# Both one-hots of an edge-to-node kernel made by bf16 matmuls of integer rows and one ScalarE Relu each

## The reference

```python
q, k, v = x @ Wq + bq, x @ Wk + bk, x @ Wv + bv
e = edge_attr @ We
k_e, v_e = k[src] + e, v[src] + e
alpha = einsum(q[dst], k_e) / sqrt(16)            # per head
attn = softmax of alpha over the edges of one dst
out = segment_sum(attn * v_e, dst)
x_r = x @ Wskip + bskip
beta = sigmoid([out, x_r, out - x_r] @ Wbeta)
out = beta * x_r + (1 - beta) * out
return layernorm(x + x + relu(layernorm(out) * gamma + beta_ln))
```

## Time and profile before

| | |
|---|---|
| median of three executions | 2535.12 us |
| span of the profiled execution | 2124.7 us |
| so outside the span, by the median | 410.4 us |
| busy: PE, DVE, ACT, POOL | 74%, 85%, 53%, 71% of the span |
| DMA engines busy, mean | about three quarters of the main loop |

### The profile page before, as it was taken

The page is one execution under the profiler, slowest core; times in us unless marked ns, Lnnn a source line. Parts: engine busy times, 40 slices in busy tenths (PEclk is TensorE's granted clock), DMA queues, the critical chain, the costliest instruction groups (busy, mean ns, idle before and its releaser), DMA issues. The chain is left out here.

```text
span 2124.7 us, 43320 instructions
## 1 busy us (share of the span) xinstructions
PE 1580.3 (74%) x10903; PEld 1429.2 (67%) x10903; DVE 1807.1 (85%) x3704; ACT 1121.3 (53%) x3755; POOL 1502.4 (71%) x1586
## 2 busy tenths in 40 slices
PE   7678788778776777777776777777777777877763
PEld 5577777668676666666675776667666767767652
DVE  6687787788878888888888898898898999999985
ACT  1154445445445545555555555566555665666656
POOL 0377777777777777777777777777777777777750
PEclk9898899998999999999999989999999999899985
DMA  8887787777777777777777777777777777777741
GB/s 297 280 246 233 233 240 235 236 233 236 222 215 212 218 216 214 222 211 218 221 215 225 216 223 217 222 226 221 215 223 225 226 224 228 224 226 219 228 128 36
DMA packets 298207, 467.63 MB, mean 220 GB/s; under 512 B 49766, under 2 KB 192826, under 8 KB 297862
## 3 DMA queue, kind: packets, MB, share of 16 engines
q1 hardware_dynamic: 222552, 259.24, 39.7%
q0 software_dynamic: 75408, 205.58, 33.7%
HBM read 413.96 MB, written 50.66 MB: 219 GB/s over the span
## 5 line engine op out<-in xcount | busy, mean ns | idle before, releaser
L742 POOL DMA_INDIRECT kv<-kv_tab,src_all x1498 | 1425.4, 952 | 480.9 <-issue 443.4
L851 PE MATMUL e_ps<-we,ea 128*128 128x128 f32 x3136 | 472.2, 301 | 278.4 <-DVE kve L1437 271.8
L851 PEld LDWEIGHTS e_ps<-we,ea 128*128 128x128 f32 x3136 | 417.7, 208 | 324.5 <-DVE kve L1437 175.6
L1437 DVE TENSOR_TENSOR kve<-kv,e_ps 128x768 f32<-128x768 f32 (+1 forms) x392 | 421.6, 1084 | 214.8 <-DMA kv<-kv_tab,src_all 214.0
L1095 ACT ACTIVATE dist_en<-iota_n,neg_rel 128x128 bf16<-128x128 f32 x1568 | 500.0, 396 | 46.3 <-issue 46.3
L1119 ACT ACTIVATE wt_ps<-logit,used_b 128x64 f32<-128x64 f32 x196 | 62.3, 318 | 831.3 <-issue 692.0
L969 PE MATMUL sum_ps<-wv,hot_en 128*128 128x136 f32 x3136 | 466.4, 303 | 11.8 <-DVE wv L1487 4.6
L969 PEld LDWEIGHTS sum_ps<-wv,hot_en 128*128 128x128 f32 x3136 | 429.7, 209 | 31.9 <-issue 31.9
L864 PE MATMUL q_ps<-q_win,hot_ne 128*128 128x128 f32 x3136 | 420.6, 292 | 0.9 <-DMA q_win<-q_tab 0.9
L864 PEld LDWEIGHTS q_ps<-q_win,hot_ne 128*128 128x128 f32 x3136 | 407.3, 210 | 1.2 <-DMA q_win<-q_tab 1.2
L1458 DVE TENSOR_REDUCE logit<-prod 128x64 f32<-128x1024 f32 x196 | 239.2, 1220 | 19.4 <-issue 0.4
(11 more groups left out here) (144 smaller groups left out, 1237.9 us busy)
## 6 DMA issues: line engine op xcount, KB each, us to landing
ea<-eaT SPq DMA_DIRECT2D x196, 512.0 KB
row_b<-rel_row SPq DMA_DIRECT2D x196, 256.0 KB
q_win<-q_tab SPq DMA_DIRECT2D x392, 64.0 KB
kv<-kv_tab,src_all POOLq DMA_INDIRECT x1498
sum_tab<-sums SPq DMA_DIRECT2D x391, 59.5 KB
kv_tab<-tab_buf SPq DMA_DIRECT2D x33, 384.0 KB, 3.7
logit<-sum_tab SPq DMA_DIRECT2D x49, 136.0 KB
xt_buf<-xT SPq DMA_DIRECT2D x33, 192.0 KB, 4.0
```

The costliest lines, as they stand in the source:

```text
L742: pool.indirect_dma_start(out=head_rows(q) if u == t == 0 else kv[:, s, t, :], out_offset=None, in_=kv_tab[:, :], in_offset=bass.IndirectO ...
L851: mm = pe.matmul(e_ps[u][:, t * P:(t + 1) * P], ea[:, par, (u * TILES_G + t) * P:(u * TILES_G + t + 1) * P], we[:, :], start=True, stop=True)
L1437: dve.tensor_tensor(kve[:, s, a:TILES_G, :, :], kv[:, s, a:TILES_G, :].rearrange("p t (a c) -> p t a c", a=2), e4[:, a:TILES_G, :, :].to_b ...
```

## The change

Nothing of the result changes; the one-hots are made in another way. With r the relative number of an edge and n the number of a node, 1 - (r - n)^2 is 1 where they agree and at most 0 elsewhere, so its Relu is the one-hot. It is made by matmuls of bf16 rows whose products are exact: r, and r^2 in two parts (`rel_tab`, three rows in HBM in place of one), with two rows of ones below (`rel5`), against five rows of n (`node5`).

- `nearness(q,u)`: one matmul 3x128 by 3x512 into `q_ps[u]`, after `products(q-1,u)` has read that bank. `node_one_hot` moves to ScalarE: Relu of `q_ps` with a bias in a column (`near_b`) into `hot_ne`, which has two buffers for four. `q_spread` then overwrites the bank.
- `edge_nearness(q,u)`: four matmuls 5x128 by 5x128 into `e_ps[u]`, after `keys_values(q,u)` has read it. `edge_one_hot` is one Relu of `e_ps`. `edge_part(q+1,u)` waits for that Relu, no longer for `kve`.
- VectorE loses `node_one_hot`; ScalarE loses its Abs operations; `load_row` brings 3x1024 numbers in place of a broadcast to 128 partitions. Its buffer is read last by `edge_nearness`, so `load_row(q+1)` waits for `edge_nearness(q-1)`; before it waited for `node_one_hot(q-1)`, which VectorE made in step q-3.
- In the table stage ScalarE squares `rel_rows` twice, VectorE makes the rest (`rel_lo`) and the node rows, SyncE stores three rows for one.

```diff
             def load_row(q):
                 if q >= 2:
-                    sp.wait_ge(hotne_ok, 2 * q - 2)
-                sp.dma_start(row_b[:, q % 2, :], rel_row[:, q * PAIR:(q + 1) * PAIR].to_broadcast([P, PAIR])
-                             ).then_inc(row_ld[q % 2], 16)
+                    sp.wait_ge(near_ok, 2 * q - 2)
+                    sp.wait_ge(dist_mm, 2 * q - 2)
+                sp.dma_start(rel3[:, q % 2, :], rel_tab[:, q * PAIR:(q + 1) * PAIR]).then_inc(row_ld[q % 2], 16)
...
+            def nearness(q, par, u, i):
+                g = 2 * q + u
+                if u == 0:
+                    pe.wait_ge(row_ld[par], 16 * (i + 1))
+                if q:
+                    pe.wait_ge(prod_ok, g - 1)
+                pe.matmul(q_ps[u][:, :], node3[:, :], rel3[:, par, u * EDGES_G:(u + 1) * EDGES_G], start=True, stop=True
+                          ).then_inc(near_ok, 1)
+
+            def edge_nearness(q, par, u):
+                g = 2 * q + u
+                pe.wait_ge(kve_ok, kve_count(g))
+                for t in range(TILES_G):
+                    mm = pe.matmul(e_ps[u][:, t * P:(t + 1) * P],
+                                   rel5[:, par, (u * TILES_G + t) * P:(u * TILES_G + t + 1) * P], node5[:, :],
+                                   start=True, stop=True)
+                mm.then_inc(dist_mm, 1)
...
                 if not last:
                     for u in range(2):
+                        edge_nearness(q, par, u)
+                    for u in range(2):
                         edge_part(q + 1, 1 - par, u, i + par, False)
+                        nearness(q + 1, 1 - par, u, i + par)
...
             def edge_one_hot(q, par, u, reuse):
                 g = 2 * q + u
-                act.wait_ge(disten_ok, g + 1)
+                act.wait_ge(dist_mm, g + 1)
                 if reuse:
                     act.wait_ge(sum_ok, g - 3)
-                act.activation(hot_en[:, 2 * par + u, :, :], dist_en[:, u, :, :], ACT.Relu, bias=1.0, scale=-1.0
+                act.activation(hot_en[:, 2 * par + u, :, :].rearrange("p t n -> p (t n)"), e_ps[u][:, :], ACT.Relu
                                ).then_inc(hoten_ok, 1)
+
+            def node_one_hot(g):
+                act.wait_ge(near_ok, g + 1)
+                if g >= 2:
+                    act.wait_ge(q_ok, g - 1)
+                act.activation(hot_ne[:, g % 2, :], q_ps[g % 2][:, :], ACT.Relu, bias=near_b[:, :]).then_inc(hotne_ok, 1)
...
-                edge_distance(q, 0, first == 0)
-                edge_one_hot(q, par, 0, first is None or first >= 2)
-                edge_distance(q, 1, first == 0)
+                for u in range(2):
+                    edge_one_hot(q, par, u, first is None or first >= 2)
                 unit_part(q)
+                if q + 1 < PAIRS:
+                    for u in range(2):
+                        node_one_hot(2 * q + 2 + u)
...
                 weights(q, par, q - LAG + 1 if first is None else 1, first is None or first >= 2)
-                edge_one_hot(q, par, 1, first is None or first >= 2)
...
                 weighted(q, par, reuse)
-                if ahead:
-                    node_one_hot(q + 2, par, i + 1)
                 unit_part(q)
```

More of the change, by code:

```diff
@@ L188, in build @@
         ea = sb("ea", [P, 2, 2 * EDGES_G])
-        row_b = sb("row_b", [P, 2, 2 * EDGES_G], BF16)
+        rel5 = sb("rel5", [BOTH_K, 2, 2 * EDGES_G], BF16)
+        rel3 = rel5[0:NEAR_K, :, :]
+        node5 = sb("node5", [BOTH_K, P], BF16)
+        node3 = node5[0:NEAR_K, :]
+        node_near = sb("node_near", [BOTH_K, P])
+        node_hi = sb("node_hi", [BOTH_K, P], BF16)
+        node_two = sb("node_two", [BOTH_K, P])
+        pick = sb("pick", [BOTH_K, 4])
+        node_sq = sb("node_sq", [P, 1])
+        near_b = sb("near_b", [P, 1])
         q_win = sb("q_win", [P, 4, C])
-        hot_ne = sb("hot_ne", [P, 4, EDGES_G])
-        dist_en = sb("dist_en", [P, 2, TILES_G, P], BF16)
+        hot_ne = sb("hot_ne", [P, 2, EDGES_G])
         hot_en = sb("hot_en", [P, 4, TILES_G, P])
@@ L248, in build @@
         g_put = sb("g_put", [P, 1], I32)
+        rel_sq = kve[0:PAIRS // 2, 0:2, :, :, :].rearrange("p s t a c -> p (s t a c)")
+        rel_hi = hot_en[0:PAIRS // 2, 0:2, :, :].rearrange("p s t n -> p (s t n)").bitcast(BF16)
+        rel_lo = hot_en[0:PAIRS // 2, 2:4, :, :].rearrange("p s t n -> p (s t n)").bitcast(BF16)
         dst_rows = logit[0:PAIRS // 2, 0:2 * PAIR].bitcast(I32)
@@ L282, in build @@
         eps_b = sb("eps_b", [P, 1])
-        near_b = part(EDGES_G // 2).bitcast(BF16)
         q_ahead = part(Q_ROUNDS, TB, C)
@@ L347, in build @@
         hotne_ok = sem("hotne_ok")
-        disten_ok = sem("disten_ok")
+        dist_mm = sem("dist_mm")
         negm_ok = sem("negm_ok")
@@ L351, in build @@
         denom_ok = sem("denom_ok")
-        rowid_ok = sem("rowid_ok")
+        square_ok = sem("square_ok")
+        node3_ok = sem("node3_ok")
+        near_ok = sem("near_ok")
         sums_ok = sem("sums_ok")
@@ L529, in _ @@
                 if r == 10:
-                    sp.wait_ge(row_cast, 1)
-                    sp.dma_start(rel_row.rearrange("one (p j) -> (one p) j", j=2 * PAIR), rel_rows[:, :]
-                                 ).then_inc(rel_st, 16)
+                    for k, rows in enumerate((rel_rows[:, :], rel_hi, rel_lo)):
+                        sp.wait_ge(row_cast, k + 1)
+                        sp.dma_start(rel_tab[k:k + 1, :].rearrange("one (p j) -> (one p) j", j=2 * PAIR), rows
+                                     ).then_inc(rel_st, 16)
             def load_nodes(r):
@@ L988, in _ @@
             with pe.If(grouped):
+                pe.wait_ge(node3_ok, 2)
                 for u in range(2):
+                    nearness(0, 0, u, 0)
                     edge_part(0, 0, u, 0, True)
                 for u in range(2):
-                    q_spread(0, 0, u, 0, True)
+                    q_spread(0, 0, u, 0)
+                for u in range(2):
+                    edge_nearness(0, 0, u)
                 for u in range(2):
                     edge_part(1, 1, u, 0, False)
+                    nearness(1, 1, u, 0)
                 biases_made()
@@ L1077, in _ @@
             act.copy(neg_rel[:, :], dst_all[:, :]).then_inc(cast_ok, 1)
+            act.wait_ge(row_cast, 1)
+            act.activation(rel_sq, rel_rows[:, :], ACT.Square).then_inc(square_ok, 1)
+            act.activation(rel_hi, rel_rows[:, :], ACT.Square).then_inc(row_cast, 1)
             act.wait_ge(first_mm, 1)
@@ L1244, in step @@
                 weights(q, par, q - LAG + 1 if first is None else 1, first is None or first >= 2)
-                edge_one_hot(q, par, 1, first is None or first >= 2)
             with act.If(grouped):
+                act.wait_ge(rel_st, 16 * NEAR_K)
+                act.wait_ge(node3_ok, 2)
+                for u in range(2):
+                    node_one_hot(u)
                 for q in range(ROUND):
@@ new lines, in _ @@
+            dve.wait_ge(square_ok, 7)
+            dve.scalar_tensor_tensor(node_two[:, :], node_hi[:, :], pick[:, 1:2], node_two[:, :], ALU.mult, ALU.add
+                                     ).then_inc(square_ok, 1)
+            dve.wait_ge(square_ok, 8)
+            dve.scalar_tensor_tensor(node5[:, :], node_near[:, :], pick[:, 2:3], node_two[:, :], ALU.mult, ALU.add
+                                     ).then_inc(node3_ok, 1)
+            dve.wait_ge(row_cast, 2)
+            dve.tensor_tensor(rel_lo, rel_sq, rel_hi, ALU.subtract).then_inc(row_cast, 1)
@@ L1587, in unit_part, with step @@
                     mix(u)
-            def step(q, par, i, first=None, ahead=True):
+            def step(q, par, i, first=None):
                 reuse = first is None or first >= 2
@@ L1602, in step @@
                 weighted(q, par, reuse)
-                if ahead:
-                    node_one_hot(q + 2, par, i + 1)
                 unit_part(q)
             with dve.If(grouped):
-                dve.tensor_copy(row_id, part_id[:, :]).then_inc(rowid_ok, 1)
-                dve.wait_ge(rowid_ok, 1)
-                for q in range(2):
-                    node_one_hot(q, q, 0, False)
                 for q in range(ROUND):
@@ L1632, in _ @@
                 for q in range(PAIRS - ROUND, PAIRS):
-                    step(q, q % 2, q // 2, ahead=q + 2 < PAIRS)
+                    step(q, q % 2, q // 2)
                     if q == PAIRS - 3:
```

66 lines of the change are left out of this document (37 added, 29 removed).

## The result

The changed kernel takes 3254.8 us, median of four executions (3243.8 to 3276.7), against 2534.8 us before: a ratio of 1.285, 95% interval 1.280 to 1.290. The prediction was 2550 us, with 2578 as its upper end. The sign was right; the time was wrong by 700 us.

The account below looks back on a forecast made before the run. GpSimd's gathers were taken to bound the kernel from first to last. Table stage +5, main-loop removals 0, new loop +11, step 194 +1.1, VectorE's end -1.5: +15.6, taken as +15 on 2535.1, 2550 us; range 2537 to 2578.

Parts of the forecast that it names:

- Outside the span lie 410.4 us, which I leave as they are: Whole kernel: 410.4 us of the 2535.1 us median lay outside the 2124.7 us span and were left unchanged.
- the cover of 8.7 us: Main loop: VectorE can be some 8.7 us late before a gather waits, at no cost except at the end.
- if the time outside the span moves: Stated sign of being wrong: the 410.4 us outside the span would change; no size was given.
- Table stage: Before the gathers: added VectorE work and stores cost +5 us, between +1 and +8; first gather at 85 us for 79.8.
- Gathers, +0: Main loop: last gather's start less the first stays 1962 us; above 1975 the loop would be the bound for long.
- Behind the last gather: End of the kernel: the end comes 94 us after the last gather's start, where it was 82.7 us.
- The places in a step: Main loop, from T, the start of `products(q,0)`: Exp at T + 4.0, `weighted` at T + 4.45, `top_row` at T + 6.6.
- The half clock: TensorE's loop: two sets of work at half clock now stand on the path, about +0.3 us a step.
- the forecast's own case: Steps 166 to 193 take 10.45 us through TensorE and ScalarE, +11 us late at the end; 2550 us, chance 0.44.
- TensorE's loop is the bound for long: Rival, chance 0.24: 43 steps with `make_queries` at 10.6 us give +12, the last 28 +22, table +5: 2574 us.
- The rival by occupancy: Rival, chance 0.02: VectorE, the engine with the highest occupancy, is the bound; each 1.21 us saved counts, 2300 us.
- I am wrong if the clock rises: Stated sign of being wrong, on TensorE in the main loop: its clock rises; no size was given.

## Why the prediction was wrong, and where it was right

**The step that failed: "Outside the span lie 410.4 us, which I leave as they are".** They were inside. The page showed an execution in which signals were prompt, the times came from executions in which they were late, and I took a difference of 19% for a fixed cost. With it went the first sentence, that GpSimd is held from the first gather to the last, and the cover of 8.7 us: in the timed executions GpSimd waited for TensorE at each pair (2.25 us at 1502.28). The prediction named the sign ("if the time outside the span moves") but did not price it.

**Where the 720 us come from.** Before, with late signals, a pair is 8.76 us from the first to the last start of its eight gathers, 0.94 for the last one, 1.84 until VectorE gets its signal, and 0.45 to the next gather: 11.99. `edge_part`, for which VectorE waits, and `q_spread`, for which GpSimd waits, were done by then; only their signals were missing. After, `hot_ne` on ScalarE needs the signal of `nearness`, and `q_spread` can only start behind it: 8.74 + 0.95 for the gathers, 1.74 to the signal, 0.84 until TensorE begins, 3.62 of `q_spread` at half clock, 0.26 to the next gather: 16.15. The difference is 4.2 us in the pair read, of which the hand-over is 0.84 and `q_spread` 3.62 (1.95 to 2.05 at full clock, so some 1.6 are the clock). 720 / 196 = 3.7 on the mean of all pairs. Shown are the lateness in rows of gathers, that it goes with plain loads, and that pace shortens it; the division in hand-over and clock is read from one pair.

**The steps held against the run with prompt signals** (span 2179.4 us, +54.7 on the page of before, for the forecast +15; the job's own executions of the kernel before have spans of 2114.0 to 2123.2):

- Table stage, +5 (1 to 8): the first gather starts at 89.1 for 79.8 us, +9.3, above its range. But it starts at 85.3 to 89.1 us in all runs of the changed kernel whose first gathers are indirect and at 78.3 to 81.1 in those of the kernel before, so about +7: at the upper end of the range.
- Gathers, +0: last less first start 1998.2 for 1962.2, +36.0. Above the 1975 that I had set as the mark of the rival, but not as that rival has it (below).
- Behind the last gather, 94 us for 82.7: it was 92.1 (2179.4 - 2087.3), +9.4. Right as a number, in part by luck: since the gathers did wait, this is about the used-up cover of 8.7 us, and not 11 us of lateness that the cover had hidden.
- The durations: Relu 0.596 and 0.687 for 0.59 and 0.67; four matmuls of `edge_nearness` 0.39 for 0.45; `nearness` 0.39, in its bounds. By the rule of the Trainium skill, page "ScalarE: Activation LUTs", section "What ACT_TABLE_LOAD costs", an estimate for the two Relus is 0.61 and 0.71 us. The trace lies between that and mine.
- The places in a step: with T = 1504.07 in the rows below, Exp is at T + 3.96 for T + 4.0, `weighted` at T + 4.71 for T + 4.45, `top_row` at T + 6.13 for T + 6.6.

```profile
1504.07 1.27 DVE L1521 TENSOR_TENSOR prod<-q_ps,kve 128x512 f32<-128x512 f32 x2
...
1508.03 0.31 ACT L1159 ACTIVATE wt_ps<-logit,used_b 128x64 f32<-128x64 f32 x1
...
1508.78 1.22 DVE L1559 TENSOR_TENSOR wv<-kve,wt_ps 128x1024 f32<-128x1024 f32 x1 [1.37 <-ACT wt_ps L1159]
...
1510.20 0.27 PE L904 MATMUL max_ps<-ident,top 128*1 128x128 f32 x1 [0.50 <-ACT used_b L1150]
```

- The half clock, "about +0.3 a step", is the term that was mis-sized; its working had no count of how often such a step comes. At 1950 us one step has full clock in its first half and half clock in its second:

```profile
1950.12 1.16 PE L866 MATMUL e_ps<-we,ea 128*128 128x128 f32 x8
...
1951.53 2.07 PE L866 MATMUL e_ps<-we,ea 128*128 128x128 f32 x8
1953.53 0.60 PE L877 MATMUL q_ps<-rel,node 3*128 3x512 bf16 x1
1954.06 3.78 PE L895 MATMUL q_ps<-q_win,hot_ne 128*128 128x128 f32 x16
```

Against 1.16, 0.39 and 2.05 in a step at full clock this one is 2.85 us longer, all of it in TensorE's row of work between `kve` and the next queries. So steps at the end are longer than the 10.45 us I took. `products` starts nine times from 1983.52 to 2073.75 us, 8 steps of 11.28 us:

```profile
1983.52 1.28 DVE L1521 TENSOR_TENSOR prod<-q_ps,kve 128x512 f32<-128x512 f32 x2
...
2073.75 1.28 DVE L1521 TENSOR_TENSOR prod<-q_ps,kve 128x512 f32<-128x512 f32 x2
```

From 1504.07 to 1595.72 it is 9 steps of 10.18 us. Over steps 166 to 193 the mean is 11.25 us: 28 x 1.2 = 34 us beyond the gathers' 10.05, where the forecast had 11. Taken two by two (a step with a unit and one without), they are 20.6 us long in the middle where TensorE had no half clock (three of them) and 23.6 where it had about 7 us of it (seven); in the kernel before it is 19.8 us without, 20.6 with about 3 us and 20.1 with about 7, so there the half clock lay beside the path, as the prediction says.

What happened is therefore the forecast's own case with a term three times as large, and not the rival "TensorE's loop is the bound for long". That one had +12 us from the 43 steps with `make_queries`, at 10.6 us each. Steps 10 to 44 took 10.00 us each, and up to pair 155 the gathers are no later than in the kernel before; all of the 36 us come behind it. The rival by occupancy (VectorE, 2300 us) fell: without VectorE's one-hot the kernel was slower on either kind of chip.

- "I am wrong if the clock rises": with prompt signals its mean was 0.936 for 0.917, and it was no help; with late ones it fell to 0.742 for 0.782.

## What to carry over

In this case a span 410 us below the measured times was not a fixed cost but a sign that the page and the times are of different executions: when span and time differ by more than a few us, run the kernel before again before anything is argued from its page. A step that is taken off one engine and given to two others as a hand-over and back is not paid by its length alone, but by all that lies on the way: the latency of the signals, and the clock at which the waiting engine goes on; here two Relus of 0.6 us and some small matmuls replaced 1.2 us of a VectorE that mostly had time, and cost 3% at best and 28% where signals are late. And when an engine waits in such a loop, price the work behind the wait at half clock as well.

## What was not expected of the hardware

- TensorE's signals can come microseconds late while indirect gathers follow one another: from the fourth gather in a row on in most cases (table above), until 1.6 to 1.8 us after the last one's end. With plain loads of the same bytes there is none of it on the same kind of chip (2135 us beside 2525 for before, 2004 beside 2603). What it is that holds them is not shown by any run here.
- It was so in three jobs on three chips and not in two others on two more (2120 us). The timed executions of the kernel before were of the first kind and its page of the second. The traces of the first kind also hold far fewer semaphore changes for the same kernel (15,417 against 57,053 on the page of before), so the recording may have a part in it; this is open.
- A 0.31 us memset behind each gather made the kernel before 1.9% faster where signals were late. In the changed kernel the same memset brought the ratio from 1.285 to 1.065. Where signals were prompt, the pace of 1.43 us was itself the bound (2409 us).
